# A recommendation network on one core: chunk 0's grams made by whole-array products, its start-up loads regrouped, one gram copy a burst

## What is computed

```python
dots = jnp.einsum('bfd,bgd->bfg', bottom_output, bottom_output)      # 2048 samples, 27 features of 128
pairs = dots[:, _TRIL_I, _TRIL_J]                                    # 351 products of different features
x = jnp.concatenate([bottom_mlp_output, pairs, pad], axis=1)         # 128 + 351 + 1 = 480
for w, b in ((w0, b0), (w1, b1), (w2, b2), (w3, b3)):                # 480 -> 1024 -> 1024 -> 512 -> 256
    x = jax.nn.relu(x @ w.T + b)
return x @ w_out.T + b_out
```

## Time and profile before

| | |
|---|---|
| median of 3 runs | 504.66 us (503.03 to 505.19) |
| profiled execution | 504.3 us, with a span of 502.2 us |
| busy | PE 481.4 us, DVE 169.6, ACT 163.1, POOL 132.5 |
| the chain that ended last | PE 84%, DMA 9%, SP's queue 4% |
| DMA | 53.88 MB, 107 GB/s on average |

### The profile page before, as it was taken

The page is one execution under the profiler, slowest core; times in us unless marked ns, Lnnn a source line. Parts: engine busy times, 40 slices in busy tenths (PEclk is TensorE's granted clock), DMA queues, the critical chain, the costliest instruction groups (busy, mean ns, idle before and its releaser), DMA issues.

```text
span 502.2 us, 18573 instructions
## 1 busy us (share of the span) xinstructions
PE 481.4 (96%) x7595; PEld 467.5 (93%) x7595; DVE 169.6 (34%) x384; ACT 163.1 (32%) x380; POOL 132.5 (26%) x242
## 2 busy tenths in 40 slices
PE   6776998999999999999999999999999999999998
PEld 5565998998999999999999999999999999999997
DVE  1145635444331542134322432144312533031100
ACT  3244633424222342224232342234231432233112
POOL 1540221122312232233222232223212332224221
PEclk9679899999999999999999999999999999999999
DMA  8995877757676646754565656754675563300000
GB/s 204 259 314 143 232 143 115 114 106 124 101 115 122 108 78 99 130 102 78 85 106 114 114 87 102 129 104 76 97 112 121 87 101 62 74 29 2 1 0 1
DMA packets 281091, 53.88 MB, mean 107 GB/s; under 512 B 265126, under 2 KB 279230, under 8 KB 281022
## 3 DMA queue, kind: packets, MB, share of 16 engines
q1 hardware_dynamic: 279090, 52.22, 55.1%
q10 hardware_dynamic: 1932, 0.61, 0.5%
HBM read 45.71 MB, written 7.09 MB: 105 GB/s over the span
## 4 chain that ended last, share of the span: by engine, by line
PE 84%; DMA 9%; SPq 4%; DVE 1%; ACT 1%; issue 1%; ACTq 0%; DVEq 0%
PE acc L671 73%; PE gram_ps L629 8%; DMA rows<-in_r_bottom_output_dram 4%; DMA blocks<-grams 3%; DMA pairs<-blocks 2%; SPq L442 2%; SPq L424 1%; PE gram_ps L597 1%; PE side_ps L602 1%; DVE xt L844 1%; PE side_ps L597 1%; SPq L389 1%; PE acc L602 1%; PE side_ps L692 0%; SPq L394 0%
## 5 line engine op out<-in xcount | busy, mean ns | idle before, releaser
L671 PE MATMUL acc<-h_a,w_hi 128*128 128x256 f32 x1152 | 217.5, 286 | 0.0
L671 PEld LDWEIGHTS acc<-h_a,w_hi 128*128 128x128 f32 x1152 | 182.0, 191 | 1.6
L763 ACT ACTIVATE h_full<-acc,small_t 128x256 f32<-128x256 f32 x175 | 82.8, 474 | 260.3 <-PE acc L671 259.6
L671 PE MATMUL acc<-h_a,w_lo 128*128 128x256 f32 x576 | 158.6, 283 | 0.0
L542 POOL TENSOR_TENSOR h_a<-h_full,h_a 128x256 fp32r<-128x256 f32 x96 | 72.1, 751 | 173.7 <-DVE h_a L856 173.7
L671 PEld LDWEIGHTS acc<-h_a,w_lo 128*128 128x128 f32 x576 | 110.3, 192 | 0.0
L671 PE MATMUL acc<-x,w_hi 128*128 128x256 f32 x504 | 97.3, 288 | 5.0 <-ACT x L773 5.0
L671 PE MATMUL acc<-h_b,w_hi 128*128 128x256 f32 x512 | 95.3, 284 | 0.0
L542 POOL TENSOR_TENSOR h_b<-h_full,h_b 128x256 fp32r<-128x256 f32 x64 | 47.2, 737 | 174.2 <-DVE h_b L856 174.2
L671 PEld LDWEIGHTS acc<-x,w_hi 128*128 128x128 f32 x504 | 81.2, 194 | 6.2 <-ACT x L773 5.9
L671 PEld LDWEIGHTS acc<-h_b,w_hi 128*128 128x128 f32 x512 | 80.9, 192 | 0.0
(11 more groups left out here) (54 smaller groups left out, 178.2 us busy)
## 6 DMA issues: line engine op xcount, KB each, us to landing
rows<-in_r_bottom_output_dram SPq DMA_DIRECT2D x444, 64.0 KB, 2.1
blocks<-grams SPq DMA_DIRECT2D x30, 216.0 KB, 3.8
w_raw<-in_L_rec_w_dram SPq DMA_DIRECT2D x6, 1024.0 KB, 8.0
early_rows<-in_r_bottom_output_dram SPq DMA_DIRECT2D x12, 224.0 KB, 6.3
stage_pairs<-in_L_rec_w_dram SPq DMA_DIRECT2D x1, 1408.0 KB, 11.7
w_raw<-in_L_rec_w_dram SPq DMA_DIRECT2D x2, 512.0 KB, 7.7
mlp_rows<-r_bottom_mlp_output_dram SPq DMA_DIRECT2D x8, 128.0 KB, 2.2
pairs<-blocks SPq DMA_DIRECT2D x8, 126.0 KB
```

What stands on the lines that cost most here:

```text
L671: last = nc.tensor.matmul(acc_slot(c, slot), weight(wp, layer, m, k), in_tile(layer, k, xp), start=(k == 0 and n == 0), stop=(k == K_TILES ...
L763: nc.scalar.activation(h_full[:, slot % 2, :], acc_slot(c, slot), ACT.Relu, bias=small_t[:, slot:slot + 1]).then_inc(drained, 1)
```

## The change

Six things change, nearly all of them before chunk 1.

- **Loads of x.** Chunk 0's 16 units come in six loads (1, 1, 2, 4, 4 and 4 units). A partition now holds four consecutive rows of 128 values, so that a piece is 2 KB where it was 512 bytes. W0 is one load (`stage_w0`), behind all of x, where its pairs' columns were loaded ahead of unit 9.
- **Chunk 0's grams.** `gram_early` makes one product of 108 x 108 of each group of four samples, with all of its cross terms: four matmuls a unit in place of 16. Since rows now lie in another order, `early_copy` puts them right while it copies. VectorE copies the whole result, 108 x 432 in place of 128 x 108, into the room of W1 in `w_raw`. The spills take only the four blocks on the diagonal (`spill_early`), each 27 x 27 runs of 256 bytes.
- **W1 to W3** are loaded by ScalarE, since W1's room is taken until the spills have landed: W1's first half behind chunk 0's `pairs_hi`, its second at hook 8, W2 and W3 at hook 20. All 26 of their groups are turned inside chunk 0's products, at hooks 4, 6, 8, ... 54, through two banks of `gram_ps`.
- **W0's order**: GpSimd keeps two thirds of the copies, VectorE takes the others behind its last gram move.
- **ScalarE's gathers** of chunk 0 stand behind the fifth group of W0 and no longer behind all of them. SP waits for the gathered pairs before it loads chunk 1's rows.
- **Steady work**: four units of grams share a bank, and ScalarE copies a burst by one instruction of 128 x 432 in place of four of 128 x 108. Chunk 1's units move to hooks 8, 13, ... 48, chunk 2's first to 50 and 56.

```diff
-ACC_RING, GRAM_RING, TURN_RING = 3, 4, 2
-XT_RING, XT_LAG = 8, 2
+ACC_RING, GRAM_RING, TURN_RING = 3, 4, 4
+XT_RING, XT_LAG, BURST, UNIT_BANKS = 8, 2, 4, 2
-W1_EARLY, FIRST_UNIT, LATE_HOOK = 7, 6, 22
-AHEAD, AHEAD_HOOK = 2, 48
+GATHER_AT, W1_HOOK, FIRST_UNIT, LOAD_HOOKS = 4, 4, 8, (8, 20)
+AHEAD, AHEAD_HOOK = 2, 50
+EARLY_LOADS = [(0, 1), (1, 1), (2, 2), (4, 4), (8, 4), (12, 4)]
...
-    for n in range(BEFORE_CHUNK + W1_EARLY, LATE_WEIGHTS):
-        hooks[n - BEFORE_CHUNK - W1_EARLY].append(("weights", n))
+    for n, place in enumerate(LOAD_HOOKS):
+        hooks[place].append(("load", 1 + n))
+    for n in range(BEFORE_CHUNK, W_GROUPS):
+        hooks[W1_HOOK + 2 * (n - BEFORE_CHUNK)].append(("weights", n))
...
-        steps += [("weights", BEFORE_CHUNK + n) for n in range(W1_EARLY)] + [("pairs", 0)]
+        steps += [("pairs", 0), ("load", 0)]
...
+        def spill_early(engine, s):
+            at = slice(FEATS * s, FEATS * (s + 1))
+            engine.dma_start(blocks[0:FEATS, :, s * RUN:(s + 1) * RUN], early_grams[at, at]).then_inc(spilled, 16)
...
+            def load_early(i):
+                u, n = EARLY_LOADS[i]
                 if u >= EARLY_SLOTS + ROWS_RING:
-                    sp.wait_ge(turned, u - EARLY_SLOTS - ROWS_RING + 1)
-                sp.dma_start(early_rows_of(u)[0:FULL_ROWS], x_full[0, u]).then_inc(early_loaded[u], 16)
+                    sp.wait_ge(turned, u + n - EARLY_SLOTS - ROWS_RING)
...
+                src = bass.AP(x.tensor, u * step_u, [[UNIT_GROUPS * DIM, FULL_ROWS], [step_u, n], [1, UNIT_GROUPS * DIM]])
...
-            for i in range(3):
-                load_weights(1, w1, 2 * i, 2 * i + 2, w1_loaded[i])
             spill(0, (0, 1))
             gather(0, PIECES[0::2])
-            load_weights(1, w1, 6, 8, w1_loaded[3])
+            for t in range(3):
+                sp.wait_ge(gathered[t], 16 * PIECES_OF[t])
...
+            def gram_early(u):
+                pe.wait_ge(xt_done, u + 1)
+                if u >= GRAM_RING:
+                    pe.wait_ge(grams_done, u + 1 - GRAM_RING)
+                for j in range(UNIT_GROUPS):
+                    last = nc.tensor.matmul(early_gram(u)[:, j], early_group(u, j), early_group(u, j), start=True, stop=True)
+                last.then_inc(gram_done, 1)
...
-                nc.scalar.activation(gram_place(u), gram_found(u), ACT.Copy).then_inc(grams_done, 1)
+                nc.scalar.activation(gram_place(u), gram_found(u), ACT.Copy).then_inc(grams_done, BURST)
...
+            def load_late(n):
+                if n < 2:
+                    for i in (2 * n, 2 * n + 1):
+                        load_weights(1, w1, 2 * i, 2 * i + 2, w1_loaded[i])
+                else:
+                    for i in range(2):
+                        load_weights(2, w2, 2 * i, 2 * i + 2, w2_loaded[i])
+                    load_weights(3, w3, 0, 2, w3_loaded)
...
+            def order_w0():
+                dve.wait_ge(w0_loaded, 16)
+                ordered = raw_rows(0)[:, :, DIM:]
+                for col, n, q, step in ROW_RUNS[2::3]:
+                    last = nc.vector.tensor_copy(ordered[:, :, q:q + (n - 1) * step + 1:step], stage_w0[:, :, DIM + col:DIM + col + n])
+                last.then_inc(w0_in_order, 1)
```

125 lines of the change are left out of this document (63 added, 62 removed).

## The result

The changed kernel took 506.15 us in the median of 20 runs (502.86 to 510.56), the kernel before on the same chip 503.79 (501.62 to 506.37). The ratio is **1.0050**, with a 95% interval from 1.0028 to 1.0072: slower, by about the half per cent that such a comparison can tell. (One of the 20 runs, the one of 510.56, was in the chip's slower state and is left out of the ratio.) The profiled span is 504.2 us against 502.2.

The account below looks back on a forecast made before the run. PE, busy 96% of the span, bounds the kernel; the rest is the start-up chain up to T0. 504.3 - 7.9 (T0) + 3.1 (W1 groups) + 2.0 (W1 wait) - 1.7 (rows wait) = 499.8 us, range 494.5 to 507.

Parts of the forecast that it names:

- T0: First product on chunk 0's last pairs tile, after the start-up: forecast at 41.5 us instead of 49.37, gain 7.9.
- Spills: Start-up step writing out chunk 0's grams: 7.4 us forecast for 2916 runs of 256 bytes, between 5.9 and 8.6.
- rival 4: Start-up spills use only nine DMA engines and take 9.5 us, kernel time 501.4; chance 4 in 10, inside the forecast's range.
- the sum: Whole kernel: the forecast's terms added to the old profiled execution of 504.3 us, giving 499.8.
- Seven groups among the products: Behind T0: seven groups of W1, once hidden in the gather's shadow, stand among the products and cost +3.1 us.
- W1's first half: Behind T0: this load takes 5.8 us and PE waits 1.4 for it; +2.0 us in all, from 0.6 to 5.5.
- the further 0.6: Behind T0: extra 0.6 us for a PE clock that may fall during the wait for W1.
- -1.7 ... I expect this wait to go: Behind T0: the old 1.68 us PE wait at 76.90, through VectorE, for chunk 1's rows would vanish, -1.7 us.
- rival 2: Behind T0: PE waits over 5 us for W1, rows and weights delay each other; 504 to 505 us, chance 0.14.
- or nothing if the late loads slow the rows: Behind T0: reservation that the -1.7 us gain is lost if late W1 and W2 loads slow chunk 1's rows.
- Chunk 1's pairs: At chunk 1's pairs: the old 0.98 us wait stays, so 0 change.
- Steady part: From 130 us on, PE busy without a gap; one copy a burst relieves only ScalarE, so 0 change.

Follow-up runs that it names:

- e2: Changed kernel with W1's second half loaded right behind its first, not at hook 8: 506.38 us, ratio 1.0035.
- e4: Changed kernel with W1's second half, W2 and W3 loaded in SP's queue behind or between chunk 1's rows, not ScalarE's: 506.11 us, ratio 1.0040.
- e5: Changed kernel with chunk 0's grams made by the old small 32 x 27 products and with the old spills: 511.41 us, ratio 1.0129.
- e12: e1 with three of chunk 0's four spills taking 32 partitions (864 runs) instead of 27: 500.22 us, ratio 0.9939.
- e9: e5 with two more whole-array 108 x 108 products a unit, results thrown away: 510.02 us, ratio 1.0148.
- e1: Changed kernel with W2 and W3 loaded by SP behind the start-up's small loads, before the spills, not at hook 20: 500.62 us, ratio 0.9912.
- e11: Changed kernel, wide grams in room of W1's second half and W2; W1's first half and W3 loaded before spills, the others at T0, hooks 15, 24: 500.12 us.
- e6: e5 with all of W1, W2 and W3 issued by ScalarE behind its two spills of chunk 0: 514.57 us, ratio 1.0193.
- e8: Kernel before with only the steady work changed: four units of grams share a bank, one ScalarE copy a burst: 502.87 us, ratio 0.9977.
- e7: e6 with W0 issued ahead of the last load of x: 514.32 us, ratio 1.0190.
- e10: e1 with W1's third quarter loaded at hook 8 and its fourth at hook 17: 501.29 us, ratio 0.9944.

## Why the prediction was wrong

The time lies inside the range (494.5 to 507.0). The sign is wrong: I gave 0.70 to faster and 0.12 to slower, and the kernel is 6.4 us above the forecast.

- **T0: right, with luck in it: errors inside it cancel.** 41.33 for 41.5. PE's start, the turns, the grams (0.76 for four against 0.8), their end (26.6 against 27.0) and the clock (rise at 9.5 against 10) all hold. VectorE's copy was mis-sized (0.92 for 0.65), but after the last gram it counts once. W0 landed at 24.0 and not at 20, since x ahead of it came at about 250 GB/s and not at 368; GpSimd, which I had done at 28.0, ended at 32.2; VectorE, which I had done at 31.7, ended at 30.5. So W0 was ordered at 32.2 for 31.7, by the other engine. And one trace is not exact to a tenth: e2 and e4, which are the same program up to there, issued the spills at 29.16 and 29.14 instead of 27.55 and had T0 at 41.78 and 41.66.
- **Spills: rival 4's mechanism, but not its price.** 8.0 us, where the sum had 7.4 and the rival 9.5. The share stood at 0.60 to 0.77 in 30 to 34 us, where 864 runs a spill held 0.87 to 1.07 (e5, 36 to 40 us) and 1.00 (e12, 30 to 31 us). The Trainium skill (DMA: Bandwidth & Descriptors, "Why a DMA increments its semaphore by 16 and not by 1") has this rule, that a transfer spreads over the largest number up to 16 that divides the slowest dimension on both of its sides; by it 729 runs from 27 partitions give nine engines and 864 from 32 sixteen. The shares agree with it roughly, since nine of sixteen is 0.56. That the nine engines cost anything is not shown: e5's 864 runs with nothing beside them took the same 8.0 us and e9's 6.5, and the 729 of e1 and e11 took 7.5.
- **Seven groups among the products: +3.1**, unchanged.
- **W1's first half: right.** The first load took 5.4 (5.8 in the sum) and PE stood for 1.43 (1.4 in the sum). The clock did not fall there, so the further 0.6 was not needed.
- **The step that failed: "-1.7 ... I expect this wait to go".** The old wait for rows did not go. It became two, 3.50 and 3.96, 7.46 us together. The term was -1.7 and measured +5.8 (7.46 - 1.68), with the remainder of 1.65 on top, which I put down to the slow clock and which the sum didn't have: 9.1 us of error. The other terms gave 2.6 back (T0 0.1, W1 0.6, pairs 1.0, steady 0.9), which leaves 6.5: the span is 504.2, and the forecast's 4.5 us of gain from 502.2 make 497.7. I counted what SP must *issue* (0.53 a load) against PE's pace at the hooks, from a row with little else in flight. What decides is how long the rows take to *land* and how fast SP can issue while megabytes pass. The earlier trace rows had 8.42 for sixteen; the trace of before also had 14.02 for the sixteen from 41.60 on, with W1's fourth quarter just ahead of them, and I did not take that row. I also left out that the need for the rows would come 8 us earlier with T0 while SP's start stayed where it was; e6 shows that this does no harm as long as no weights are in flight. I priced W1's delay by rows beside it (8.9) but not the rows' delay by W1. I had named the mechanism, in rival 2 and in the clause "or nothing if the late loads slow the rows"; I bounded its price at zero gain and not at a loss.
- **Chunk 1's pairs: 0 in the sum, -0.98 measured.** The spill is at 106.22 instead of 102.32, and at 119.06 PE comes later still.
- **Steady part: 0 in the sum, -0.9 measured** (2.94 late at 123.47, 2.0 at the end), in line with e8 alone (-1.2).

Rival 2 was the nearest case, at 504 to 505 and 0.14. Its second half is what came, rows and weights that delay each other at the hooks, through SP and VectorE. Its first half did not: it wanted over 5 us of PE's wait for W1, and PE stood for 1.43. And it priced the rows' part at 1.7, where it measured 7.5 against the sum.

What stays open: the exact size of the slow clock's part (1.7 to 2.8); what in the chip makes rows and weights delay each other, whose effect alone the runs show; which products bring PE's clock up, of which e5 and e9 show one pair; and what it would give to let SP start chunk 1's rows before the gathered pairs are there, which no run tried.

## What to carry to other kernels

Before a load is moved behind a start-up, ask what small loads will be in flight beside it, and price **their** landing time, not only its own. Look in the trace for the same small load with the large one beside it. A wait of one engine for another (here PE for VectorE) may be a queue effect twice removed: follow it to the DMA that the second one stands before. And a gain of 8 us on the chain that sets T0 is worth nothing by itself if the work that was hidden in the shadow of that chain now stands in the open.

## What the runs showed of the hardware

- **Small products and PE's pace.** With turns between them, 32 x 27 products in four quarters of the array left a turn at 0.98 us in all of e5's units up to 31.32 us (1.49 us a unit) and in most of those of e6, e7 and the kernel before, also where PE was busy without a gap (e5, 22 to 32 us); e6 has the granted clock at 0.50 beside that duration. 108 x 108 products on the whole array (after: 1.13 a unit), or the small ones plus two such fillers (e9: 1.28, of which 0.47 filler), had it at 0.54 to 0.59 from about 10 us on, in e9 with a slow spell after a pause. That four times the multiplications make the start-up shorter I had not expected.
- **Issuing is not free of traffic.** Sixteen 64 KB loads in SP's queue took 8.30 us with no weights beside them (e6), 13.57 and 14.38 with 2 MB in ScalarE's queue (e4, e11), 17.06 with 3 MB (e10), and 19.12 and 19.31 with 4 MB (after, e1). The landing time of such a load went from 2.2 us to 8 to 9.
- **729 against 864 runs.** A share of 0.60 to 0.77 of the DMA engines, against 0.87 to 1.07 of them, and yet no clear difference from issue to the wait's end: 7.5 to 8.0 us against 6.5 to 8.0.
- **The rate of a load.** In the start-up x came at 242 GB/s in 2 KB pieces, and W0 at 393 in pieces of 1920 bytes.
- **The column of the granted clock can miss a stretch.** It reads 1.00 in 20 to 30 us of e5, where each turn takes the 0.98 us that stands beside 0.50 in e6.
